# Token lists of 64 experts: built by one-hot matmuls, or scattered by indirect DMA as the positions become known

## The reference

```python
logits = x @ gate_w
probs = jax.nn.softmax(logits.astype(jnp.float32), axis=-1)
w, idx = jax.lax.top_k(probs, TOP_K)                       # TOP_K = 8 of 64
w = w / jnp.sum(w, axis=-1, keepdims=True)
...
pos = jnp.take_along_axis(jnp.cumsum(onehot, axis=0) - 1, e_flat[:, None], axis=1)[:, 0]
slot = jnp.minimum(pos, CAPACITY)                          # CAPACITY = 128
buf = jnp.zeros((E, CAPACITY + 1, H), x.dtype).at[e_flat, slot].set(x[tok])
gu_e = jnp.einsum('ech,ehf->ecf', buf, expert_gate_up_w)
act = _silu(gu_e[..., :I]) * gu_e[..., I:]
out_e = jnp.einsum('eci,eih->ech', act, expert_down_w)
y = out_e[e_flat, slot] * w_flat[:, None]
y = jnp.where((pos < CAPACITY)[:, None], y, jnp.zeros_like(y))
```

## Time and profile before

| | |
|---|---|
| median of 3 runs | 1431.49 us (1423.39 to 1431.89) |
| the profiled execution: time | 1429.87 us |
| its span in the profile | 1428.1 us |
| busy share of the span | TensorE 80%, VectorE 58%, ScalarE 52%, GpSimd 27% |
| mean granted TensorE clock | 0.883 of full speed |
| stage 1, stage 2, stage 3 | to about 451 us, to about 857 us, to the end |

### The profile page before, as it was taken

The page is one execution under the profiler, slowest core; times in us unless marked ns, Lnnn a source line. Parts: engine busy times, 40 slices in busy tenths (PEclk is TensorE's granted clock), DMA queues, the critical chain, the costliest instruction groups (busy, mean ns, idle before and its releaser), DMA issues.

```text
span 1428.1 us, 18332 instructions
## 1 busy us (share of the span) xinstructions
PE 1148.7 (80%) x6049; PEld 842.0 (59%) x6049; DVE 823.9 (58%) x2068; ACT 739.4 (52%) x1469; POOL 380.0 (27%) x320
## 2 busy tenths in 40 slices
PE   4788888787774667999699961769888888989887
PEld 3354543543333456888588861637766666767566
DVE  4386687777765554455645434657565565755342
ACT  2786677777862643556656521343443435334521
POOL 3011011011000001566556552103323242321422
PEclk9697999999996999999999995597989998999988
DMA  8214414504103103677557745330403123020000
GB/s 251 78 63 118 115 60 118 173 18 128 51 34 138 71 1 95 157 164 178 169 141 168 187 71 142 98 93 2 112 20 89 43 70 93 17 60 3 15 15 15
DMA packets 89900, 129.77 MB, mean 91 GB/s; under 512 B 20496, under 2 KB 59792, under 8 KB 89552
## 3 DMA queue, kind: packets, MB, share of 16 engines
q1 hardware_dynamic: 77520, 109.73, 25.8%
q0 software_dynamic: 12288, 18.88, 7.6%
HBM read 72.18 MB, written 30.70 MB: 72 GB/s over the span
## 4 chain that ended last, share of the span: by engine, by line
PE 58%; DVE 17%; ACT 10%; issue 5%; DMA 3%; SPq 3%; POOL 3%; POOLq 0%; ACTq 0%; DVEq 0%
PE psum L911 8%; PE psum L741 6%; PE psum L652 5%; PE psum L817 4%; PE psum L629 3%; PE psum L757 3%; PE psum L846 3%; PE psum L776 3%; PE psum L647 3%; PE psum L898 3%; POOL hidden L1668 3%; SPq L1725 2%; PE psum L826 2%; PE psum L618 2%; DVE weights L1281 2%
## 5 line engine op out<-in xcount | busy, mean ns | idle before, releaser
L629 PE MATMUL psum<-q_stack,k_stack 96*128 96x512 f32 (+1 forms) x256 | 130.2, 525 | 70.9 <-ACT weights L1124 29.3
L1616 POOL TENSOR_SCALAR vareps<-moments 128x4 f32<-128x4 f32 x32 | 8.3, 260 | 517.0 <-DVE moments L1183 517.0
L1668 POOL TENSOR_TENSOR hidden<-hidden_whole,hidden 128x512 fp32r<-128x512 f32 x64 | 83.8, 1316 | 203.0 <-DVE hidden L1569 203.0
L1521 DVE TENSOR_REDUCE peaks<-psum 128x2 f32<-128x308 f32 x256 | 105.5, 468 | 46.1 <-PE psum L848 46.0
L1649 POOL DMA_INDIRECT expert_sums<-made,sum_rows x64 | 102.9, 1607 | 101.2 <-DVE made L1491 85.2
L846 PE MATMUL psum<-k_stack,q_stack 96*128 96x256 f32 x256 | 97.6, 443 | 33.9 <-DMA q_stack<-q_stage 11.0
L911 PE MATMUL psum<-w_con_high,hidden 128*128 128x256 f32 x512 | 114.2, 322 | 10.6 <-POOL hidden L1668 10.5
L629 PEld LDWEIGHTS psum<-q_stack,k_stack 96*128 96x128 f32 (+1 forms) x256 | 52.8, 211 | 116.9 <-DVE weights L1281 46.7
L652 PE MATMUL psum<-weights,values 128*32 128x512 f32 x512 | 106.4, 701 | 10.3 <-DVE weights L1281 10.3
L1124 ACT ACTIVATE weights<-psum 128x512 f32<-128x512 f32 x160 | 88.9, 602 | 47.9 <-PE psum L632 23.9
L1281 DVE SCALAR_TENSOR_TENSOR weights<-psum,weights 128x512 f32<-128x512 f32 x160 | 107.1, 679 | 5.4 <-ACT weights L982 5.0
(11 more groups left out here) (187 smaller groups left out, 2646.2 us busy)
## 6 DMA issues: line engine op xcount, KB each, us to landing
q_stack<-q_stage SPq DMA_DIRECT2D x192, 128.0 KB, 2.4
expert_w<-in_expert_w SPq DMA_DIRECT2D x64, 384.0 KB
expert_sums<-zeros SPq DMA_DIRECT2D x6, 1408.0 KB, 7.1
fetched<-expert_sums SPq DMA_DIRECT2D x16, 512.0 KB, 4.6
wk_stack<-in_wk SPq DMA_DIRECT2D x16, 384.0 KB, 3.8
rows_scratch<-rows SPq DMA_DIRECT2D x8, 640.0 KB, 3.4
k_raw<-in_k SPq DMA_DIRECT2D x16, 300.0 KB
x<-in_x SPq DMA_DIRECT2D x8, 512.0 KB, 6.7
```

Of the source, the lines that this page charges most:

```text
L629: T.matmul(to, k[0:row, head, :], q[0:row, head // 2, :], start=True, stop=True).then_inc(scored, 1)
L1521: V.tensor_reduce(peaks[h % 2][:, t, 2 * p:2 * p + 2], view, AX.X, ALU.max).then_inc(wide.frees(key, i), 1)
L1668: G.tensor_tensor(hidden[k % BURST][:, 1, :], whole[n % 2][:, :], hidden[k % BURST][:, 0, :].bitcast(F32), ALU.subtract).then_inc(hid_spli ...
```

## The change

The lists are now in DRAM as 8192 words, `list_scratch[position * 64 + expert]`, filled beforehand with the number of a spare row. `count` makes from the position and the expert's number the place in that array, multiplies by the mask, takes the eight largest of each token (`slot_top`) and casts them to `slots`. A new unit `slot(h, t, k)` on GpSimd writes, by one indirect DMA of 128 indices, the tokens' numbers (`ids`) of tile `t` to the places of their `k`-th pick; indices of 8192 and more are skipped. That is 32 DMAs for a half, 256 in all. Those of halves 0 to 5 run in stage 1, two for each chunk, two halves after their own (`listing`); the 64 of halves 6 and 7 stand at the start of stage 2. Then SP loads the lists as `tokens`. `hots`, `place`, `lists` and their tiles are gone. `back` takes 14 steps and `fusing` 28 between `tokens` and the loop. `set_ids` makes the constants early in stage 1. The rows gathered get a zeroed spare part, so that one list of indices serves reads and writes.

```diff
+def slot_steps(h):
+    picks = [("slot", h, t, k) for t in range(HT) for k in range(TOPK)]
+    return [picks[i:i + 2] for i in range(0, len(picks), 2)]
...
-    plan += [("load_rest",), ("load_x", 1)]
+    plan += [("load_rest",), ("ids",), ("load_x", 1)]
...
             late.drain()
+            listing.drain()
+            if h >= 2:
+                listing.add(("slots", h - 2), slot_steps(h - 2))
...
         late.step()
+        listing.step()
+    listing.drain()
     late.drain()
...
-    back.step()
-    plan.append(("hots", 0))
-    for i in range(TILES):
-        if i + 1 < TILES:
-            plan.append(("hots", i + 1))
-        plan.append(("place", i))
-        if i % 2 and i > 4:
-            back.step()
-    plan.append(("lists",))
-    back.step(3)
+    plan += [("slot", h, t, k) for h in (HALVES - 2, HALVES - 1) for t in range(HT) for k in range(TOPK)]
     plan.append(("tokens",))
+    for n in range(14):
+        back.step()
+        fusing.step(2)
...
                 elif k == 0:
                     T.wait_ge(exp_in, 16)
-                    T.wait_ge(tokens_set, 1)
...
             def count(h):
...
-                V.scalar_tensor_tensor(picked[:, :, :], masks[:, :, :], -FAR, counts, ALU.mult,
+                V.scalar_tensor_tensor(picked[:, :, :], counts, float(EXPERTS),
+                                       numbers[:, :].unsqueeze(1).to_broadcast([P, HT, EXPERTS]), ALU.mult,
                                        ALU.add).then_inc(misc.frees(key), 1)
                 V.wait_ge(*misc.freed(key))
-                V.tensor_scalar(picked[:, :, :], picked[:, :, :], FAR, None, ALU.add).then_inc(dve_own, own.up())
+                V.tensor_tensor(picked[:, :, :], picked[:, :, :], masks[:, :, :], ALU.mult).then_inc(dve_own, own.up())
...
+                for t in range(HT):
+                    m = V.max(slot_top[:, t, :], picked[:, t, :])
+                m.then_inc(dve_own, own.up())
+                if h >= 2:
+                    V.wait_ge(listed[h % 2], 16 * HT * TOPK * (h // 2))
                 V.wait_ge(dve_own, own.n)
+                V.tensor_copy(slots[h % 2][:, :, :], slot_top[:, :, :]).then_inc(slots_set, 1)
+
+            def set_ids():
+                V.wait_ge(digits_in, 32)
+                by_row = digits[:, :, 0].unsqueeze(2).to_broadcast([P, NA, NA])
+                by_column = digits[:, :, 0].unsqueeze(1).to_broadcast([P, NA, NA])
+                V.scalar_tensor_tensor(numbers[:, :].rearrange("p (a b) -> p a b", b=NA), by_row, float(NA), by_column,
+                                       ALU.mult, ALU.add)
+                V.tensor_scalar(lane[:, :], spare_row[:, :], float(-TOKENS), None, ALU.add)
+                V.tensor_copy(spare_list[:, :], spare_row[:, :].to_broadcast([P, EXPERTS])).then_inc(dve_own, own.up())
                 V.wait_ge(dve_own, own.n)
+                V.scalar_tensor_tensor(ids_f[:, :], numbers[:, 0:TILES], float(P), lane[:, :].to_broadcast([P, TILES]),
+                                       ALU.mult, ALU.add).then_inc(dve_own, own.up())
                 V.wait_ge(dve_own, own.n)
+                V.tensor_copy(ids[:, :], ids_f[:, :]).then_inc(ids_set, 1)
...
+            def slot(h, t, k):
+                if (t, k) == (0, 0):
+                    if h == 0:
+                        G.wait_ge(list_filled, 16)
+                    G.wait_ge(slots_set, h + 1)
+                i = HT * h + t
+                G.indirect_dma_start(list_dram, bass.IndirectOffsetOnAxis(ap=slots[h % 2][:, t, k:k + 1], axis=0),
+                                     ids[:, i:i + 1], None, bounds_check=CAP * EXPERTS - 1,
+                                     oob_is_err=False).then_inc(listed[h % 2], 16)
...
             def gather(e):
                 if e == 0:
-                    G.wait_ge(tokens_set, 1)
+                    G.wait_ge(tokens_in, 16)
...
+            def fill_lists():
+                S.dma_start(digits[:, :, :], D["a_iota"][:, 0, :, :]).then_inc(digits_in, 16)
+                S.dma_start(spare_row[:, :], D["spare_row"]).then_inc(digits_in, 16)
+                S.wait_ge(ids_set, 1)
+                S.dma_start(list_dram.rearrange("(p e) o -> p (e o)", p=P), spare_list[:, :]).then_inc(list_filled, 16)
...
+                    S.dma_start(rows_dram[TOKENS:, 0:DIM], zeros[:, 0, :]).then_inc(sums_clear, 16)
+                    S.dma_start(rows_dram[TOKENS:, DIM:ROW], zeros[:, 0, 0:EXPERTS]).then_inc(sums_clear, 16)
...
+            def load_tokens():
+                for i in range(2):
+                    S.wait_ge(listed[i], 16 * HT * TOPK * HALVES // 2)
+                S.dma_start(tokens[:, :], list_dram.rearrange("(p e) o -> p (e o)", p=P)).then_inc(tokens_in, 16)
```

More of the change, by code:

```diff
@@ L168, in plan_first @@
     plan += [("load_x", k) for k in range(h, HALVES)]
-    early, late = Stream(plan), Stream(plan)
+    early, late, listing = Stream(plan), Stream(plan), Stream(plan)
     needed, later = {}, {}
@@ L786, in turn_up @@
                 m.then_inc(fused.fills(key), 1)
-            def place(i):
-                T.wait_ge(hot_a_set, i + 1)
-                T.wait_ge(hot_b_set, i + 1)
-                for g in range(4):
-                    for part in (1, 2):
-                        m = T.matmul(bank[g][:, 0:NB * EG], hot_a[i % 3][:, part, g, :, :],
-                                     hot_b[i % 3][:, :, EG * g:EG * g + EG], start=i == 0 and part == 1,
-                                     stop=i == TILES - 1 and part == 2)
-                m.then_inc(placed, 1)
-            def list_tokens():
-                T.wait_ge(list_in, 64)
-                T.transpose(bank[4][:, 0:EXPERTS], by_expert[:, :], ident[0:EXPERTS, 0:EXPERTS]).then_inc(placed, 1)
             def turn_got(e):
@@ L918, in tensor_program @@
                      "project_o": project_o, "turn_rows": turn_rows, "gate": gate, "count": count,
-                     "sh_up": sh_up, "sh_down": sh_down, "inside": inside, "turn_up": turn_up, "place": place,
-                     "tokens": list_tokens, "turn": turn_got, "gate_up": gate_up, "down": down,
+                     "sh_up": sh_up, "sh_down": sh_down, "inside": inside, "turn_up": turn_up, "turn": turn_got, "gate_up": gate_up, "down": down,
                      "turn_q1": turn_q1, "peak": peak, "peaks": turn_peaks, "scores1": scores1,
@@ L1161, in scalar_program @@
                      "matrix": stage_matrix, "inside": inside, "across": across, "turn_up": turn_up,
[L1162 removed]
+                     "turn": turn_got, "gate_up": gate_up, "key_split1": key_split1,
                      "turn_q1": turn_q1, "peaks": turn_peaks, "exp1": exp1, "weigh1": weigh1,
@@ L1585, in vector_program @@
                      "sh_inner": sh_inner_, "sh_down": sh_down, "matrix": stage_matrix, "across": across,
-                     "hid_bias": set_hid_bias, "out_bias": set_out_bias, "hots": hots, "lists": set_lists,
-                     "tokens": set_tokens, "gate_up": gate_up, "down": down, "add_experts": add_experts,
+                     "hid_bias": set_hid_bias, "out_bias": set_out_bias, "ids": set_ids, "gate_up": gate_up, "down": down, "add_experts": add_experts,
                      "key_split1": key_split1, "turn_q1": turn_q1, "peak": peak, "peaks": turn_peaks,
@@ L1677, in gpsimd_program @@
             assert set_.n == POOL_FIRST
-            units = {"rstd": norm_rstd, "bias_x": bias_x, "load_rest": scale_bias, "gather": gather, "down": scatter,
+            units = {"rstd": norm_rstd, "bias_x": bias_x, "load_rest": scale_bias, "slot": slot, "gather": gather, "down": scatter,
                      "add_experts": add_experts, "bias_out": bias_out, "up": hidden_rest}
@@ L1832, in sync_program @@
                      "load_expert": load_expert, "sh_load": sh_load, "sh_weights": sh_weights,
-                     "hid_bias": load_con, "lists": send_lists, "fetch": fetch, "load_k1": load_k1,
+                     "hid_bias": load_con, "tokens": load_tokens, "ids": fill_lists, "fetch": fetch, "load_k1": load_k1,
                      "load_v1": load_v1, "send_q1": send_q1, "peaks": turn_peaks, "out": out_tile}
```

112 lines of the change are left out of this document (25 added, 87 removed).

## The result

The changed kernel took **1484.31 us** (median of 4, 1479.10 to 1485.19), the kernel before 1430.40 beside it: a ratio of 1.0355, 95% interval 1.0314 to 1.0396, so slower. The profiled execution took 1484.12 us, its span is 1482.3, at a mean granted clock of 0.854.

A forecast was written before the change was run, and what follows sets the result against it. TensorE (91% busy) was taken to bound the experts' stretch; in attention no engine was full. Start 3, attention 8, stage 2 19 and clock 3 gave +33 on 1429.9 us: 1463, or 1464 as median; range 1410 to 1505.

The forecast's parts named there:

- (b): GpSimd's queue: 256 slot DMAs added, each taken at 1.31 us like an indirect read, bounds 0.6 and 1.9.
- Rival 1: Slots without an index in bounds are nearly free, 0.6 us each: 1414 us in all; chance 0.17.
- rival 2: A slot costs what an accumulating write does, 1.9 us, so GpSimd bounds attention: 1575 us; chance 0.12.
- (c, d): Start of stage 2: 64 slot DMAs take 84 us with nothing covering them; stage 2 ends 19 us later.
- (d): Stage 2: `feats_m` waits behind `tokens` on SP, then 40.1 us of TensorE work, 44 at 91%; +19 us.
- (e): Clock: after idling some 90 us in stage 2, TensorE's matmuls start at granted level 0.50; +3 us.
- Rival 3: The 14 + 28 steps do run under stage 2's slots, returning 33 us: about 1428; 0.04 with other small-result ways.
- (f): Attention: 192 slots, two to a step, delay `rstd` queued behind them on GpSimd; +8 us, of 0 to 14.
- (g): Kernel start: VectorE's `set_ids` waits for two small loads ahead of its first `stats`; +3 us.
- The rule weighed: VectorE and GpSimd share a locked port pair; could slow attention's slots to 2.33 us; nothing added to the sum.

The follow-up runs named there:

- session 2 or 3: The changed kernel run again without edit in two later sessions, on two chips: 1554.07 us, then 1559.40 us.
- two edits: Against the changed kernel: `set_ids` and list filling moved behind the prologue, 1539.06 us; 14 + 28 steps written ahead of the `tokens` load, 1530.56 us.

## Why the prediction was right, and where its sum was off

Forecast 1464 us in 1410 to 1505, measured 1484: slower, for the reasons given, with a sum of +33 where +54 came.

**Price of a slot (b), right.** 1.28 us against the 1.31 taken from the indirect read. Rival 1 (cheap without an index in bounds) and rival 2 (as dear as an accumulating write) are both refuted by one row: 966/972/1652 ns over all 256.

**64 slots, nothing covers them (c, d), right.** TensorE started 90 us after the stage's start (forecast 92), the first `got` transpose 137 us after it (forecast 136.4). The kernel without them shows the cause by itself: 73 us shorter. That the second time is so close is in part luck. An `inside` unit is two matmul instructions, not one: the earlier trace rows has 112 of them for 56 units, so a unit is 0.62 us, not 0.31, and the counts of 7 and 35 ahead of the first transpose are units. The 29 units behind the wait took 15.7 us, not 9.0. From the window view of that stretch, all engines first, then L773 alone:

```profile
581.20:628.50 47.30, 44.61 (x202) 35.35 (x203) 23.31 (x50) 28.81 (x78) 2.83 (x3) 0.96 0.17 64
581.20:628.50 47.30, 15.72 (x58) 10.10 (x58) 0.96 0.17 64
```

With 0.62 us a unit the sum of (d) would have been 49 us of work, 54 at 91%. It took 47.4 us, for TensorE was busy for 94% of it and at a clock of 0.96: two errors that nearly cancel against the 44 forecast. In all of stage 2 the slip cancels too, for 29 units more ahead are 28 fewer behind: the experts' stretch is 7 us shorter than before (276 against 283), where the count gave 2. Net, stage 2 lost 14.7 us where (d) and (e) said 22; what is left of that difference lies in the dense stretch behind the wait. The clock (e) is visible (0.50, then 0.68 in 13 us), but no run prices it alone. **Rival 3** was false as the kernel stands, by SP's order; and with the order mended it gave 4 to 7 us, not 33, in sessions in which hand-offs from TensorE were late. What the cover is worth where they are not was not run.

**Attention (f), mis-sized: 31 to 38 us against 8 (0 to 14).** The failing words are "they have no wait of their own". They have one, `slots_set`, which comes when `count` is through, and GpSimd spent 62.3 us at it. My queue had the slots of a half spread evenly from its start. In truth GpSimd got the slots of the second half only at 195.5; 14 of them are 18 us and stand ahead of the next `rstd`, which started at 215.7 (202.7 before). The second error was slack: I let VectorE run ahead of its consumers and counted half. It has little: VectorE's waits for `rstd` grew by 27.1 us (3.9 to 31.0), the stretch from the fifth to the sixteenth `rstd` by 31.3. Shown is that the early slots cost this time (without them the waits are 3.9 us again and attention ends 31 to 38 us earlier), and that 27 us of it are waits for `rstd`. That the order of the queue makes all of those 27 is argued from the rows of GpSimd; the two kernels meant to test it, memsets in the slots' places and slots behind `rstd`, each brought an effect of their own.

**Start (g), open: 1 to 8 us against 3.** The first `stats` came at 13.4, as derived (11.8 before), but by the third `rstd` the lag was 7.8 us. Moving the ids behind the prologue gave back 3 to 6 of it there. How much of it reaches the end of attention differs between two profiles without early slots (1.2 and 8.5 us at the sixteenth `rstd`).

**The rule weighed**, the Trainium skill, SBUF — State Buffer, "Who interferes with whom": leaving it out of the sum was right. No slot took 2.33 us; the longest is 1.65. It doesn't explain the late hand-offs either: ScalarE waits in them too, for TensorE, and memsets on GpSimd make none. What memsets do make is a slower VectorE: its normalizing, which reads and writes SBUF, took 0.69 us beside them in place of 0.41.

**What nobody had in the sum:** the late hand-offs. The result's profile has none of them, and its four runs agree within 0.4%; by session 2 or 3 the same kernel would have stood at 1554 to 1559, outside the range. Right by what was reasoned, and also by the luck of the session.

**Open.** Shown: with all early slots, in unbroken runs of 10 to 22, results of TensorE reach ScalarE and VectorE up to 12 us late in the rows above, and under the 64 late ones up to 16; with half of them, in runs of up to 12, waits of under 4 us remain; with slots 2.3 us apart, memsets, or plain DMAs, none. Not shown: what holds them up (the rows say when TensorE ended and when the next engine started, not which of the two was late), and why the first session of the changed kernel was free of it. That session's chip isn't known, so chip and session can't be told apart. No version here beats the kernel before.

## What to carry to other kernels

Before moving work to an idle engine's queue, write down for each piece the earliest moment it may start and what is queued behind it; an average of free time (GpSimd was 9% busy) says nothing if the work becomes ready just ahead of the one small instruction that others wait for. A DMA with a list of 128 indices has a price per instruction, 1.28 us here whatever it writes, so 256 of them are 327 us of one queue. And repeat the baseline of an experiment in each session: without the second run of the changed kernel, two edits would have been blamed for 50 us that were not theirs.

## What the runs showed of the hardware

- An indirect DMA of GpSimd with 128 indices to 4-byte places: 0.97 us, and 0.30 to the next, with nearly all (3950 of 4096 in the first half) or none of the indices in bounds; a plain one of the same column 0.54 us, with nothing to the next; an accumulating one of 1 KB rows 1.58 us.
- Dense streams of them went with late hand-offs from TensorE, by 4 to 16 us in the rows shown, in all three later sessions but not in the result's (end of attention 453.7 us without them; 492.0 in the result's, 539.7, 558.2 and 566.9 with them). In attention's rows the late results were ready 7 and 8 us into an unbroken run, and four of the waits named end within about 2 us behind its last slot. A hand-off from ScalarE to VectorE in the same stretch was prompt (508.67 to 508.71).
- Beside plain DMAs of 128 packets of 4 bytes, one after another, 384 KB loads took 7.5 and 11.2 us to land in place of 3.4 and 3.5.
- Beside memsets on GpSimd (0.52 us each) a VectorE operation from SBUF to SBUF (128x256) took 686 ns in place of 406.
